# Other PSUM banks and another order for the fills of a unit, with the query projection last

## What is computed

```
def _phi(x): return jax.nn.elu(x) + 1.0
Q = _phi(x @ Wq + bq); K = _phi(x @ Wk + bk); V = x @ Wv + bv        # 16 heads of 64
KV = KV + einsum('bhd,bhe->bhde', ki, vi);  Ks = Ks + ki              # token by token
num = einsum('bhd,bhde->bhe', qi, KV);      den = einsum('bhd,bhd->bh', qi, Ks)
out = num / (den + EPS);                    attn = out @ Wo + bo
x = x + attn(xn) + tree(xn)
```

## Time and profile before

| | |
|---|---|
| median of 3 runs | 1363.02 us |
| profiled execution, its time | 1362.36 us |
| its span | 1360.7 us |
| PE busy | 1279.9 us, 94% |
| DVE, ACT, POOL busy | 806.9, 619.5, 373.7 us |
| mean granted TensorE clock | 0.992 |
| DMA | 26.0 MB, 19 GB/s |

### The profile page before, as it was taken

One profiled execution on the slowest core, in us unless ns is written; L12 is line 12 of the kernel. 1 busy time (PEld: TensorE's weight loads), 2 busy tenths in 40 slices (PEclk: granted clock), 3 DMA queues, 4 the chain that ended last, 5 costly groups with the idle time before them and its releaser, 6 DMA issues.

```text
span 1360.7 us, 49950 instructions
## 1 busy us (share of the span) xinstructions
PE 1279.9 (94%) x22173; PEld 1117.7 (82%) x22173; DVE 806.9 (59%) x2186; ACT 619.5 (46%) x1135; POOL 373.7 (27%) x590
## 2 busy tenths in 40 slices
PE   5899999999999999899999999999999999999987
PEld 5789788897978879788897978879788787878976
DVE  4664756656476564765657566574765647566462
ACT  4453544535355253453535345353553535445351
POOL 3514132141322314133141321413223141321410
PEclk9899999999999999999999999999999999999998
DMA  6000000010000100001010000100001000000000
GB/s 209 18 3 17 18 5 31 2 33 3 10 26 2 33 3 18 18 2 33 3 28 7 10 26 3 33 3 17 19 2 33 2 19 17 10 10 3 18 2 17
DMA packets 21603, 26.00 MB, mean 19 GB/s; under 512 B 1025, under 2 KB 19728, under 8 KB 21392
## 3 DMA queue, kind: packets, MB, share of 16 engines
q1 hardware_dynamic: 21392, 22.82, 5.2%
HBM read 14.43 MB, written 8.39 MB: 17 GB/s over the span
## 4 chain that ended last, share of the span: by engine, by line
PE 77%; ACT 12%; DVE 6%; issue 3%; DMA 1%; SPq 0%; DVEq 0%
PE w_pair L638 24%; PE s_pair L650 17%; PE s_pair L638 11%; PE kv_pair L723 6%; PE s_pair L708 5%; ACT ex L405 5%; PE o_pair L762 5%; PE o_pair L748 5%; ACT ex L408 4%; DVE qT L520 3%; PE o_pair L690 3%; DVE oT L536 2%; ACT k_tok L420 2%; PE w_pair L685 2%; ACT ffn_tok L413 1%
## 5 line engine op out<-in xcount | busy, mean ns | idle before, releaser
L328 POOL TENSOR_SCALAR_AFFINE_SELECT aT<-aT 64x512 f32<-64x512 f32 x256 | 167.7, 655 | 918.5 <-ACT aT L434 910.2
L405 ACT ACTIVATE ex<-w_pair,neg_bias 128x512 f32<-128x512 f32 x256 | 176.3, 689 | 197.0 <-PE w_pair L638 194.3
L638 PE MATMUL w_pair<-xnT,wk 128*128 128x512 f32 x768 | 214.1, 414 | 1.1 <-ACT k_tok L421 0.8
L638 PE MATMUL s_pair<-wv,xnT 128*128 128x512 f32 x744 | 200.5, 408 | 0.0
L638 PE MATMUL w_pair<-xnT,wq 128*128 128x512 f32 x768 | 197.6, 393 | 0.2 <-DVE wq L241 0.2
L650 PE MATMUL s_pair<-wo,oT 128*128 128x256 f32 x1536 | 191.1, 281 | 0.0
L577 DVE TENSOR_TENSOR snaps<-kv_pair,snaps 128x65 f32<-128x65 f32 x768 | 173.4, 226 | 26.4
L650 PEld LDWEIGHTS s_pair<-wo,oT 128*128 128x128 f32 x1536 | 185.6, 189 | 0.0
L638 PEld LDWEIGHTS w_pair<-xnT,wq 128*128 128x128 f32 x768 | 144.6, 189 | 32.6 <-DVE wq L241 0.6
L434 ACT ACTIVATE aT<-s_pair 128x512 f32<-128x512 f32 x128 | 76.4, 597 | 200.5 <-PE s_pair L708 200.5
L408 ACT ACTIVATE ex<-ex 128x512 f32<-128x512 f32 x256 | 161.8, 632 | 8.1
(11 more groups left out here) (102 smaller groups left out, 1773.1 us busy)
## 6 DMA issues: line engine op xcount, KB each, us to landing
x_in<-in_L_attn_x_dram SPq DMA_DIRECT2D x16, 512.0 KB, 3.9
out_dram<-y_buf SPq DMA_DIRECT2D x32, 256.0 KB, 2.2
stage<-in_L_attn_Wv_dram SPq DMA_DIRECT2D x2, 512.0 KB, 7.9
stage<-in_L_attn_Wk_dram SPq DMA_DIRECT2D x2, 512.0 KB, 9.7
stage<-in_L_attn_Wq_dram SPq DMA_DIRECT2D x2, 512.0 KB, 10.9
stage<-in_L_attn_Wo_dram SPq DMA_DIRECT2D x2, 512.0 KB, 9.2
bv_all<-in_L_attn_bv_dram SPq DMA_DIRECT2D x1, 512.0 KB, 8.6
ffn_tok<-in_L_ffn_Wq_dram SPq DMA_DIRECT2D x1, 256.0 KB
```

What stands on the lines that cost most here:

```text
L328: pool.affine_select(out=part, in_=part, compare_op=ALU.is_ge, fill=0.0, base=0, pattern=[[0, 2 * CH], [1, D]], channel_multiplier=-1).the ...
L405: act.activation(ex[:, slot], psum_of(name), ACT.Relu, scale=-1.0, bias=neg_bias[:, col:col + 1])\
L638: last = pe.matmul(dst, l, r, start=i == 0, stop=i == len(steps) - 1)
```

## The change

The list of fills gets another order and other banks. Queries move from second place to last. The unit's own oT moves from O0 to S0, and behind kT (at p = 7 it stays ahead of the y fills). V1, leaf and V0 fills that used S0 now use O1 (one V1 fill moves to S1), xT 0 moves from S1 to O0, y 0 from S0 to O1. The keys are copied by one ACT instruction in place of two, and the outer products wait for that whole copy before their first matmul in place of for its first half. No arithmetic is added or removed.

```diff
--- before.py
+++ after.py
@@ -29,28 +29,33 @@
     n = g * PAIRS + p
     ahead = divmod(n + 2, PAIRS) if n + 2 < blocks * PAIRS else None
     more = g + 1 < blocks
+    own = [(("oT", p, g), S0)]
     fills = []
     if ahead:
-        fills += [(("K", ahead[1], ahead[0]), W0), (("Q", ahead[1], ahead[0]), W1)]
-    fills.append((("oT", p, g), O0))
+        fills.append((("K", ahead[1], ahead[0]), W0))
     if p == 0:
-        fills += [(("V1", 0, g), S0), (("V1", 1, g), S1)]
+        fills += [(("V1", 0, g), O1), (("V1", 1, g), S1)]
     if p == 1:
-        fills += [(("V1", 2, g), S0)]
+        fills += [(("V1", 2, g), S1)]
     if p == 2:
-        fills += [(("V1", 3, g), S0)]
         if more:
-            fills += [(("xT", 0, g + 1), S1), (("xT", 1, g + 1), O1)]
+            fills += [(("xT", 0, g + 1), O0), (("xT", 1, g + 1), O1)]
+        fills += [(("V1", 3, g), S1)]
     if p in (3, 4):
-        fills += [(("leaf", p - 3, g), S0)]
+        fills += [(("leaf", p - 3, g), O1)]
         if more:
             fills += [(("V0", p - 3, g + 1), S1)]
     if p in (5, 6) and more:
-        fills += [(("V0", p - 3, g + 1), S0), (("gate", p - 5, g + 1), S1)]
-    if p == 7:
-        fills += [(("y", 0, g), S0), (("y", 1, g), S1)]
+        fills += [(("V0", p - 3, g + 1), O1), (("gate", p - 5, g + 1), S1)]
+    if p == PAIRS - 1:
+
+        fills += own + [(("y", 0, g), O1), (("y", 1, g), S1)]
     if ahead:
         fills.append((("kT", ahead[1], ahead[0]), W0))
+    if p < PAIRS - 1:
+        fills += own
+    if ahead:
+        fills.append((("Q", ahead[1], ahead[0]), W1))
     return fills
 
 
@@ -215,7 +220,6 @@
         xn_ready = sem("xn_ready")
         filled = [sem(f"bank{i}_filled") for i in range(6)]
         drained = [sem(f"bank{i}_drained") for i in range(6)]
-        keys_begun = sem("keys_begun")
         hi_ready = sem("hi_ready")
         relu_ready = sem("relu_ready")
         exp_ready = sem("exp_ready")
@@ -415,10 +419,8 @@
 
             def copy_keys(name):
                 act.wait_ge(filled[bank_of[name]], count_of[name])
-                half = CH // 2 * P
-                to = k_tok[:, :, :].rearrange("p c n -> p (c n)")
-                act.activation(to[:, 0:half], psum_of(name)[:, 0:half], ACT.Copy).then_inc(keys_begun, 1)
-                act.activation(to[:, half:], psum_of(name)[:, half:], ACT.Copy).then_inc(drained[bank_of[name]], 1)
+                act.activation(k_tok[:, :, :].rearrange("p c n -> p (c n)"), psum_of(name), ACT.Copy)\
+                   .then_inc(drained[bank_of[name]], 1)
 
             def high_of_output(name):
                 _, p, g = name
@@ -713,10 +715,6 @@
                 p = n % PAIRS
                 half = p // HALF
                 for t in range(CH):
-                    if t == 0:
-                        pe.wait_ge(keys_begun, n + 1)
-                    if t == CH // 2:
-                        until_drained(("kT", p, n // PAIRS))
                     for a in range(2):
                         for h in range(2):
                             off = (2 * (p % HALF) + h) * AUG
@@ -769,6 +767,7 @@
                 if p in (0, HALF):
                     for c in range(CH):
                         until_drained((f"V{p // HALF}", c, g))
+                until_drained(("kT", p, g))
                 outer_products(n)
 
             def scores_when_ready(n):
@@ -864,7 +863,7 @@
                     kind, i, g = name
                     if bank in (S0, S1) and n + 1 < UNITS:
                         pe.wait_ge(s_copied, n + 2)
-                    if bank in (O0, O1):
+                    if bank in (O0, O1) or kind == "oT":
                         pe.wait_ge(o_normed, n + 1)
                     if kind == "xT":
                         pe.wait_ge(xn_ready, g + 1)
```

## The result

The changed kernel takes 1518.63 us (median of 4 runs, 1516.81 to 1520.48) against 1362.97 us beside it: a ratio of 1.1138, 95% interval 1.1119 to 1.1158. The forecast was 1520.

What follows compares the result with a forecast made beforehand. PE, busy 94%, was taken to bound the kernel; with Q's chain exposed, 149 us over 15 blocks plus 8 in the last added 157 to 1362.36, forecast 1520 us. Range 1485 to 1565, forecast with bounds 1485 to 1555.

Steps and rivals of the forecast that it cites:

- Q's chain: Scores in 126 units: Q's 3.86 us chain against 2.45 of cover makes PE wait 1.41 us, 178 us in all.
- Fills into O0 and O1: As the unit's second fill they wait for `o_normed`, 1.95 us after K: 0.46 us exposed in five units of a block.
- kT behind K: kT's transposes can't start before 3.97 us after K; at p = 1, 3, 4 the fills between last about as long or less.
- normalise: DVE runs it at p = 0 behind Q's phi, delaying p = 1: `o_normed` at 3.28 us, kT at 4.19 after K.
- Key copy at nothing: One ACT key copy in place of two costs nothing: done 1.2 us after kT starts, outer products come at 2.5.
- Unit lengths: Forecast time of each unit p = 0 to 7, together 91.95 us a block against 82.00 before.
- The sum: Whole kernel: 149 us over 15 blocks plus 8 in the last block, +157 us on 1362.36, taken as 1520.
- The clock: Rival: PE's larger holes lower its clock; one spell a block gives 1545 us, one a unit 1700; chance 0.10.
- Q's chain was not covered: Rival at the scores' wait: Q drained within 2.45 us of its start, the 178 us vanish, 1341 us; chance 0.04.
- Early norms: Rival: `carry` not queued behind Q's phi on DVE, the 0.46 us waits vanish, some 45 us less, 1475; chance 0.06.
- my two bounds: Uncertain terms: the scores' wait, 13 us either way, and the wait for `o_normed`, -35 to +27 us.

Runs made afterwards that it cites:

- queries second: Changed kernel with Q filled right behind K again; new banks, oT behind kT and single key copy kept: 1395.39 us, ratio 1.0261.
- run 20: Not a run number: the text reads "in that run 20 stops", meaning 20 stops in the run with queries second, 1395.39 us.
- outputs third: Changed banks with the order of the kernel before (K, Q, oT into S0, others, kT) and the key copy in two halves: 1413.95 us, ratio 1.0383.
- the one before with queries last: Kernel before the change with Q moved to the end of the fills, behind kT, and nothing else: 1518.98 us, ratio 1.1184.
- the banks of p = 3 and 4 put back: Changed banks, oT third, key copy in halves, but the original's banks at p = 3 and 4: 1386.77 us, ratio 1.0187.

## Why the prediction was right

- **What bounds the kernel, and Q's chain.** Right: forecast 3.86 us from Q to scores, measured 3.86; the wait from start to start 1.31, not 1.41, since Q to `from_state` took 1.57, 0.10 more than I had put. From kT to Q it was 0.82, 0.10 more as well, which makes every unit that much longer.
- **Fills into O0 and O1.** Forecast 1.95 after K; measured 644.38 - 642.48 = 1.90. Undoing it alone gave 21 us back.
- **kT behind K.** Forecast 3.97, measured 3.98.
- **normalise.** Over-sized. In p = 1 `carry` starts later, but K's phi is not delayed:

```profile
612.22 1.66 PE L640 MATMUL w_pair<-xnT,wk 128*128 128x512 f32 x6
612.27 0.23 DVE L579 TENSOR_TENSOR snaps<-kv_pair,state 128x65 f32<-128x65 f32 x1
...
615.30 0.75 DVE L522 SCALAR_TENSOR_TENSOR kT<-w_pair,bias_one,ex 128x512 f32<-128x512 f32 x1
...
616.20 0.63 PE L687 MATMUL w_pair<-ident,kT 128*128 128x128 f32 x4 [0.92 <-DVE kT L522]
```

  kT is at 3.98 here too, where I had 4.19. I had added DVE's durations end to end; their starts overlap by up to 0.1, so that K's phi starts 3.08 after K, exactly as at p = 4.
- **Key copy at nothing.** Right, by the run with the copy in two halves.
- **Unit lengths.** Forecast 10.57, 9.83, 9.80, 9.61, 9.61, 10.44, 10.44, 21.65; measured, the usual ones, 10.56, 9.75, 9.99, 9.76, 9.76, 10.56, 10.52, 21.67.
- **The sum.** The spans differ by 156.4 us against 157 forecast, but partly by luck: I had both blocks about half a microsecond too short, which cancels, and the end of the kernel wrong. The keys' fills of the first and the last block's p = 0, of the changed kernel:

```profile
47.52 1.66 PE L640 MATMUL w_pair<-xnT,wk 128*128 128x512 f32 x6
...
1434.86 1.66 PE L640 MATMUL w_pair<-xnT,wk 128*128 128x512 f32 x6
```

  and the first of the kernel before (its last block's begins at 1282.62):

```profile
46.44 2.65 PE L638 MATMUL w_pair<-xnT,wk 128*128 128x512 f32 x6
```

  The mean block is (1434.86 - 47.52) / 15 = 92.49, not 91.95, and before (1282.62 - 46.44) / 15 = 82.41, not the 82.00 of the one block that I took. So 15 blocks lost 151 us, not 149, and the start lost 1. The last block and what follows lost 4, not 8: before, the clock fell near the end, and in the changed kernel it didn't. From K of p = 5 to the end are 36.6 us before and 33.0 after. The end of either, by windows (us; busy PE, PEld, DVE, ACT, POOL; granted clock; DMA share; GB/s), first before, then after:

```profile
1325.00:1361.00 36.00, 25.68 (x337) 23.66 (x336) 9.52 (x24) 5.46 (x10) 2.01 (x4) 0.83 0.05 16
```

```profile
1475.00:1517.00 42.00, 29.47 (x491) 25.87 (x489) 14.63 (x37) 10.32 (x17) 3.72 (x6) 1.00 0.04 14
```

- **The clock.** It didn't fall with the holes: 0.998 in the mean, above the 0.992 of before, although PE stood more. Between 120 and 1517 us there is one spell at the lower level, 0.50, in the changed kernel:

```profile
1371.60:1375.00 3.40, 3.40 (x12) 2.72 (x11) 1.06 (x3) 0.51 (x1) 0.66 (x2) 0.50 0.00 0
```

  It comes behind a wait of 1.13 us at the scores and a stop of 0.66 inside `from_chunk`; the same wait in the other units did not bring the clock down. One thing I had read wrongly: that the last block of the kernel before held the full clock. It did so behind the holes of 0.51 and 1.25, but the earlier trace rows has `from_state` at 1336.13 with 0.37 us in place of 0.27, and after two more holes, of 2.02 and 1.41 us, the clock was at the lower level:

```profile
1336.00:1345.00 9.00, 7.44 (x87) 6.87 (x88) 1.83 (x5) 0.60 (x1) 0.00 (x0) 0.50 0.01 2
```

  The changed kernel has holes of 2.32, 1.13 and 1.61 us in its last block and stays at the upper level. So the low chance of this rival came out, but the rows that I gave against it did not carry it, and what decides is open.
- **The other rivals.** `norm` did not come early, and Q's chain was not covered.
- **Slips in the working.** Early norms would have been worth 39 us by my own terms (35 in five units, 3.5 at p = 1), not 45. And my two bounds added up are 1472 to 1560, wider than the 1485 to 1555 that I called the forecast with its bounds. Neither moves the forecast.

## What to carry to other kernels

When a step is moved in an in-order engine's list, measure the whole chain from its first instruction to the one that needs its result, through every engine (here 3.86 us through ACT and DVE, neither of which is busy), and compare it with the work that stands between after the move (2.45 us forecast, 2.55 measured). Where one wait is removed, look up what the next instruction waits for: the drain of oT only moved from `from_state` to the scores. And a schedule tightened on an engine that issues many small instructions should be checked for stops that no semaphore explains.

## What the runs showed of the hardware

I had not expected stops of PE in the midst of a run of independent matmuls. In the kernel with queries second, unit 51:

```profile
586.00 0.44 PE L758 MATMUL o_pair<-v_aug,aT 64*64 64x65 f32 x14
...
588.20 0.56 PE L758 MATMUL o_pair<-v_aug,aT 64*64 64x65 f32 x18 [1.75 <-issue]
```

14 of 32 matmuls ran, then PE stood 1.75 us, and only the first of them has a semaphore to wait for. From 585 to 589 us the DMA queues carried one packet, of instructions; so the view from 585 to 587:

```profile
DMA packets 1, 0.02 MB, mean 8 GB/s; under 512 B 0, under 2 KB 0, under 8 KB 0
## 3 DMA queue, kind: packets, MB, share of 16 engines
q8 instruction: 1, 0.02, 3.5%
```

The trace has 178 such packets of 16 KB in a launch, each some 1 us long; this one landed at 586.81, and PE went on 1.39 later. In that run 20 stops of 0.9 us and more fell so: PE went on 1.26 to 1.58 after a landing. All stops of 0.6 us and more without a named releaser add up to 31 us there, of the 37 that it is slower than the kernel before, 68 us in the kernel with outputs third (38 of them at matmuls that wait for no semaphore), 2 in the changed kernel and none in the one before with queries last. The clock adds a little: five of the stops with queries second (units 21, 47, 51, 111, 115) are followed by a granted clock of 0.50, by which K and Q together take 1.5 to 1.6 us longer. In the kernel before two such stops, of 1.69 and 1.74 us, stand beside fifteen waits of 1.5 us for a drain of O1; the hole of 1.52 in the earlier trace rows is one of the fifteen. Two runs tested the cause.

**128 more instructions at the start of PE's program:**

```diff
+            for _ in range(64):
+                pe.transpose(kv_pair[:, 1, 0:2 * PAIRS], bias_rows[:, :], ident[0:2 * PAIRS, 0:2 * PAIRS])
```

> The run with queries second, and 64 more copies of a small transpose (16 rows) at the start of PE's program, 128 instructions, half of a 16 KB packet of the instruction queue. In that run PE stopped inside from_chunk and near it at units 17, 21, 28, 31, 36, 44, 47, 51 and again at 81, 85, 92, 95, 100, 108, 111, 115, 64 units later. Theory (these stops are PE running out of instructions while a packet lands, so their places depend on the count of instructions): the stops come at other units and repeat 64 units later; their sum, 30 us there, and so the time, 1395 us, may differ by 15. Rival (a data dependency or another engine stops PE): the same units.

Measured: 1394.32 us, ratio 1.0242 (1.0218 to 1.0267). The stops inside a run of small matmuls moved, to units 4, 7, 12, 19, 45, 49, 50, 53, 60, 63, 68, 76, 79, 83, 91 and 117 (the last five units of the launch apart), none of them a place of before. Four come back 64 units later (4, 12, 19, 53); the others don't, which the theory had not said. Nothing else in the kernel had changed, so the places hang on the count of instructions. The other traces say the same: the runs with queries second, with outputs third, with the banks of p = 3 and 4 put back, and with the wait of the next run all stop in units 47, 51, 95 and 123, though their spans differ by up to 89 us. The data rival falls.

**A wait in front of the scores:**

```diff
                 if more:
+                    if n >= 0:
+                        pe.wait_ge(sum_ready, sums_after[n] + 2)
                     scores_when_ready(n + 1)
```

> The run with queries second, and one wait more: the scores of unit n + 1 wait for the second sum of carry(n + 1), about 0.35 us later than they started there. Theory (a wait ahead of the densest instructions lets the instruction queue catch up): the 20 stops of 1 us and more inside from_chunk become fewer than 5, so of the 44 us that the wait adds about 27 come back: 1412 us. Rival (the stops are independent of waits ahead): they stay, 1439 us.

Measured: 1472.24 us, ratio 1.0813 (1.0783 to 1.0842). Stops at `from_chunk` fell from 25.8 us in 22 to 12.4 in 16, and to two of 1 us and more, at the same units as without the wait but shorter, as the theory has it. Fewer than 5 was right for those of 1 us and more. The time missed both numbers. PE waits 108 us for the sum, where it had waited 27 us at the scores, so the edit added 81 us and not 44: the wait is 1.89 in the unit behind `normalise` and about 0.7 in the others. So this run tells nothing by its time.

So a wait in front of the small matmuls pays a small part of itself back, here 13 of 81 us. That PE stands for want of instructions is inferred, from the landings, the places and this run; no record names it. It accounts for the tighter orders of this kernel, whose units without a stop are as short as before or shorter and which measured 1387 to 1414 us, and for the order with the long wait for Q, which has hardly a stop. Why a packet is at times asked for too late, and what would make it come earlier, was not tried.
